# Attention stage of a graph network: slot rows laid out group by group, whole-tile stores, SyncE's steps reordered, PSUM banks shared out anew

## The reference, cut to what matters

```python
q = (embeds[rows] @ qW).reshape(e, HEADS, dh)
k = (embeds[cols] @ kW).reshape(e, HEADS, dh)
v = (embeds[cols] @ vW).reshape(e, HEADS, dh)
scores = jnp.clip(jnp.einsum('ehd,ehd->eh', q, k), -10.0, 10.0)
exp_s = jnp.exp(scores)
norms = jax.ops.segment_sum(exp_s, rows, num_segments=nvar)[rows]
w = exp_s / (norms + 1e-08)
res = jax.ops.segment_sum(w[:, :, None] * v, rows, num_segments=nvar).reshape(nvar, d)
return embeds + res
```

## Time and profile before

| | us |
|---|---|
| median of 3 runs | 4100.52 (4100.29 to 4103.03) |
| profiled execution | 4099.22 |
| its span | 4097.9 |
| TensorE busy, weight loads busy | 3879.6, 3664.7 |
| VectorE, ScalarE, GpSimd busy | 1806.4, 1328.4, 518.4 |
| attention stage, from and to | about 283 to 1194 |

### The profile page before, as it was taken

One profiled execution on the slowest core, in us unless ns is written; L12 is line 12 of the kernel. 1 busy time (PEld: TensorE's weight loads), 2 busy tenths in 40 slices (PEclk: granted clock), 3 DMA queues, 4 the chain that ended last, 5 costly groups with the idle time before them and its releaser, 6 DMA issues.

```text
span 4097.9 us, 125285 instructions
## 1 busy us (share of the span) xinstructions
PE 3879.6 (95%) x46211; PEld 3664.7 (89%) x46211; DVE 1806.4 (44%) x4350; ACT 1328.4 (32%) x3904; POOL 518.4 (13%) x708
## 2 busy tenths in 40 slices
PE   3779999999979999899999999999999998999999
PEld 2669999999966665899999999999999998999998
DVE  8988999999984332322222222222222222331121
ACT  1237777777773111122222222222222221111110
POOL 1015555555530000000000000000000000000000
PEclk9989999999989999999999999999999999999999
DMA  1029999999983332555555555555555655566674
GB/s 40 3 60 216 222 220 220 219 220 222 221 212 108 108 109 81 179 203 202 204 203 201 205 202 201 205 201 202 205 201 201 207 200 192 189 219 210 212 217 145
DMA packets 525196, 746.41 MB, mean 182 GB/s; under 512 B 203503, under 2 KB 449647, under 8 KB 525036
## 3 DMA queue, kind: packets, MB, share of 16 engines
q1 hardware_dynamic: 520040, 743.21, 60.8%
q10 hardware_dynamic: 4996, 0.88, 0.1%
HBM read 620.51 MB, written 83.32 MB: 172 GB/s over the span
## 4 chain that ended last, share of the span: by engine, by line
PE 71%; DVE 9%; SPq 7%; issue 5%; DMA 5%; ACT 1%; POOL 1%; DVEq 0%; ACTq 0%; POOLq 0%
PE sum L1647 48%; PE sum L1340 19%; DMA rows<-slot_rows_d 5%; SPq L960 3%; DVE onerank L759 2%; SPq L967 1%; SPq L956 1%; DVE sc L993 1%; POOL sc L1063 1%; PE l L465 1%; SPq L943 1%; DVE qk L986 1%; PE pk L1111 1%; DVE bt L731 1%; DVE prodb L748 1%
## 5 line engine op out<-in xcount | busy, mean ns | idle before, releaser
L1647 PE MATMUL sum<-y,ring 128*128 128x192 f16 x12005 | 995.0, 246 | 4.0 <-ACT y L1496 4.0
L1647 PEld LDWEIGHTS sum<-y,ring 128*128 128x128 fp8e4 x12005 | 993.8, 98 | 4.6 <-issue 4.2
L1647 PE MATMUL sum<-u2b,ring 128*128 128x192 f16 x12005 | 993.0, 246 | 0.0
L1647 PEld LDWEIGHTS sum<-u2b,ring 128*128 128x128 fp8e4 x12005 | 992.1, 98 | 0.2
L1656 DVE TENSOR_TENSOR z<-lo,sum 128x96 f32<-128x96 f32 x441 | 112.1, 254 | 1004.5 <-ACT lo L1671 1004.0
L1111 PE MATMUL pk<-kv,hT 128*128 128x192 f16 x4900 | 486.3, 247 | 11.4 <-DVE hT L1005 9.7
L1340 PE MATMUL sum<-u,ring 128*128 128x385 f16 x2401 | 402.7, 328 | 22.2 <-ACT u L1464 22.2
L1111 PEld LDWEIGHTS pk<-kv,hT 128*128 128x128 f16 x4900 | 410.2, 99 | 12.7 <-DVE hT L1005 9.6
L1340 PEld LDWEIGHTS sum<-u,ring 128*128 128x128 fp8e4 x2401 | 235.7, 98 | 182.5 <-issue 24.6
L1192 ACT ACTIVATE kvs<-pk 128x384 f32<-128x384 f32 x735 | 313.6, 437 | 154.4 <-PE pk L1111 149.8
L1134 PE MATMUL pr<-wv,hs_wide 128*128 128x101 f32 x2450 | 323.6, 279 | 15.0 <-ACT sums L1199 13.8
(11 more groups left out here) (237 smaller groups left out, 3369.7 us busy)
## 6 DMA issues: line engine op xcount, KB each, us to landing
ring<-adjacency_t SPq DMA_DIRECT2D x490, 800.0 KB, 4.3
ring<-adjacency SPq DMA_DIRECT2D x147, 896.0 KB, 4.7
rows<-slot_rows_d SPq DMA_DIRECT2D x245, 320.0 KB, 4.0
adjacency<-row SPq DMA_DIRECT2D x147, 128.0 KB, 3.6
adjacency_t<-col SPq DMA_DIRECT2D x147, 128.0 KB, 2.6
adjacency<-row SPq DMA_DIRECT2D x49, 256.0 KB, 3.6
adjacency_t<-col SPq DMA_DIRECT2D x49, 256.0 KB, 2.4
adjacency<-row SPq DMA_DIRECT2D x49, 160.0 KB, 3.7
```

Of the source, the lines that this page charges most:

```text
L1647: m = pe.matmul(ps[r][:, 0:2 * D], w[:, t // 2, :, t % 2], n["this"][:, t, 0:2 * D], start=t == 0, stop=t == TILES - 1)
```

## The change

- Slot rows lie in DRAM and in SBUF group by group: 128 source places, then 128 destination places of a group. A chunk's load is then one run of 2560 bytes in DRAM.
- The one-hots hT are made from a pattern with gaps; reading and writing go over two halves of each group (`halves`).
- The matrices of a tile are stored whole, one DMA each for `adjacency` and `adjacency_t`, in place of five each; the transposes stay one for each chunk.
- SyncE transposes chunk c-7 (before: c-3) and stores a turned tile at lag 9 (before: its parts at lag 5); its loop has a lag of 9.
- pk has three banks in place of two, pq two in place of one. Keys and values of one third of a chunk have their own bank, and `query` waits for the score product of chunk e-2 in place of e-1.
- ScalarE copies the sums ahead of the keys and values of its step.

```diff
@@ -851,7 +851,7 @@
             x0, x1 = x_halves[h]
             n0 = 2 * x0 + i * (x1 - x0)
             eng.wait_ge(k.rows_sb.sem, k.rows_sb.at(-(-2 * x1 // 8)))
-            to = k.rows_d.rearrange("(x t) i (g e) -> t i g x e", t=2, e=P)
+            to = k.rows_d.rearrange("(x t) g i e -> t i g x e", t=2)
             for odd in range(2):
                 eng.dma_start(to[odd, i][:, x0:x1, :], k.slot_rows[odd * GROUPS:(odd + 1) * GROUPS, n0:n0 + x1 - x0, :]
                               ).then_inc(k.rows_out[h].sem, 16)
@@ -881,7 +881,7 @@
     k.weighted, k.summed = Beat(k, "at_weighted", CP), Beat(k, "at_summed", CP)
     k.q_in, k.denom, k.inverse, k.normed = (Beat(k, f"at_{x}", 2) for x in ("q_in", "denom", "inverse", "normed"))
     k.ratio, k.totalled = (Beat(k, f"at_{x}", 2) for x in ("ratio", "totalled"))
-    k.row_out, k.col_out = ([Beat(k, f"at_{x}{c}", n) for c in range(CHUNKS)] for x, n in (("row_out", 64), ("col_out", 32)))
+    k.row_out, k.col_out = ([Beat(k, f"at_{x}{b}", n) for b in range(2)] for x, n in (("row_out", 16 * CHUNKS + 16), ("col_out", 16)))
     k.out_c = Beat(k, "at_out_c", 2 * UP)
     k.av_set = k.sig("av_set")
 
@@ -894,13 +894,13 @@
 
 
     v, a, pe, pool, sp = k.v, k.a, k.pe, k.pool, k.sp
-    rows = [k.buf(ctx, f"rows{i}", [P, 2, CHUNK * P], F16) for i in range(HOMES)]
+    rows = [k.buf(ctx, f"rows{i}", [P, CHUNK, 2, P], F16) for i in range(HOMES)]
     ss = [k.buf(ctx, f"ss{i}", [P, 4, GROUPS, 2], BF16) for i in range(2)]
     high_d = [k.buf(ctx, f"high_d{i}", [P, GROUPS, HIGH_D, 2], BF16) for i in range(2)]
     low_d = [k.buf(ctx, f"low_d{i}", [P, GROUPS, LOW_D // 2, 2], BF16) for i in range(2)]
     highs, lows = k.buf(ctx, "highs", [P, HIGH_D, 2], BF16), k.buf(ctx, "lows", [P, LOW_D // 2, 2], BF16)
     q2 = [k.buf(ctx, f"q2_{i}", [P, 2, D], F16) for i in range(2)]
-    hT = [k.buf(ctx, f"hT{i}", [P, 3, CHUNK * P], F16) for i in range(2)]
+    hT = [k.buf(ctx, f"hT{i}", [P, 3, CHUNK, P], F16) for i in range(2)]
     hs = [k.buf(ctx, f"hs{i}", [P, CHUNK, P // 2, 2], BF16) for i in range(2)]
     hs_wide = [k.buf(ctx, f"hs_wide{i}", [P, CHUNK, P], F32) for i in range(HOMES)]
     hd = [k.buf(ctx, f"hd{i}", [P, CHUNK, HIGH_D, LOW_D // 2, 2], BF16) for i in range(2)]
@@ -915,10 +915,11 @@
     rowsum = k.buf(ctx, "rowsum", [P, TILES * UP], F32)
     bits = k.buf(ctx, "bits", [P, TILES * UP], I32)
     most = k.buf(ctx, "most", [P, 2], F32)
-    pq, pr = k.bank(ctx, "pq"), k.bank(ctx, "pr")
-    pk = [k.bank(ctx, f"pk{i}") for i in range(2)]
+    pr = k.bank(ctx, "pr")
+    pq = [k.bank(ctx, f"pq{i}") for i in range(2)]
+    pk = [k.bank(ctx, f"pk{i}") for i in range(3)]
     pc = [k.bank(ctx, f"pc_{i}") for i in range(2)]
-    LAG = 5
+    LAG, SENT, SP_LAG = 5, 7, 9
     last_tiles = TILES - 2 * (PAIRS - 1)
     last_chunks = last_tiles * CHUNKS
 
@@ -936,46 +937,44 @@
                 for g in range(g1 - CHUNK, g1) if g % BANK == BANK - 1 or g == GROUPS - 1]
 
     def load_rows(X, e):
-        b, i, at = e // CHUNKS, e % HOMES, (e % CHUNKS) * CHUNK * P
+        b, i, g0 = e // CHUNKS, e % HOMES, (e % CHUNKS) * CHUNK
         sp.wait_ge(k.turned.sem, k.turned.at(X, e - HOMES))
         k.settle(sp)
-        src = k.rows_d[2 * X + b, :, at:at + CHUNK * P]
-        sp.dma_start(rows[i][:], src.partition_broadcast(P)).then_inc(k.rows_in[i].sem, 16)
-
-    def parts(e):
-
-        u = units(e)
-        return e // CHUNKS, u[0][1], u[-1][1] + u[-1][2], u[-1][0]
-
-    def send(X, e):
-
-        b, g0, g1, u = parts(e)
-        c = e % CHUNKS
-        sp.wait_ge(k.out_c.sem, k.out_c.at(X, u))
+        src = k.rows_d[2 * X + b, g0:g0 + CHUNK, :, :].rearrange("g i e -> (g i e)")
+        sp.dma_start(rows[i][:].rearrange("p g i e -> p (g i e)"), src.partition_broadcast(P)).then_inc(k.rows_in[i].sem, 16)
+
+    def turn_counts(X, e):
+
+        b, u = e // CHUNKS, units(e)
+        g0, g1 = u[0][1], u[-1][1] + u[-1][2]
+        if e % CHUNKS == 0:
+            sp.wait_ge(k.col_out[b].sem, k.col_out[b].at(X, -1))
+            k.settle(sp)
+        sp.wait_ge(k.out_c.sem, k.out_c.at(X, u[-1][0]))
         k.settle(sp)
-        sp.dma_start(k.c_d[2 * X + b, :, g0 * GROUP:g1 * GROUP],
-                     flat(row[b][:, g0:g1, :]).bitcast(U8)).then_inc(k.row_out[c].sem, 16)
-        sp.wait_ge(k.col_out[c].sem, k.col_out[c].at(X, 16 * b - 1))
+        sp.dma_start_transpose(col[b][:, g0:g1, :], flat(row[b][:, g0:g1, :])).then_inc(k.row_out[b].sem, 16)
+
+    def store(X, b):
+
+        sp.dma_start(k.c_d[2 * X + b, :, :], flat(row[b][:]).bitcast(U8)).then_inc(k.row_out[b].sem, 16)
+
+    def store_turned(X, b):
+        sp.wait_ge(k.row_out[b].sem, k.row_out[b].at(X, 16 * CHUNKS + 15))
         k.settle(sp)
-        sp.dma_start_transpose(col[b][:, g0:g1, :], flat(row[b][:, g0:g1, :])).then_inc(k.row_out[c].sem, 16)
-
-    def send_transposed(X, e):
-        b, g0, g1, _ = parts(e)
-        c = e % CHUNKS
-        sp.wait_ge(k.row_out[c].sem, k.row_out[c].at(X, 32 * b + 31))
-        k.settle(sp)
-        sp.dma_start(k.t_d[2 * X + b, :, g0 * GROUP:g1 * GROUP],
-                     flat(col[b][:, g0:g1, :]).bitcast(U8)).then_inc(k.col_out[c].sem, 16)
+        sp.dma_start(k.t_d[2 * X + b, :, :], flat(col[b][:]).bitcast(U8)).then_inc(k.col_out[b].sem, 16)
 
     def sync_step(X, c, first=False, chunks=CP):
         if first and c == LAG - 1:
             sp.wait_ge(k.rows_out[1].sem, k.rows_out[1].at(64))
         for x, e in lagged(X, c, 0, first, chunks):
             load_rows(x, e)
-        for x, e in lagged(X, c, 3, first, chunks):
-            send(x, e)
-        for x, e in lagged(X, c, 5, first, chunks):
-            send_transposed(x, e)
+        for x, e in lagged(X, c, SENT, first, chunks):
+            turn_counts(x, e)
+            if e % CHUNKS == CHUNKS - 1:
+                store(x, e // CHUNKS)
+        for x, e in lagged(X, c, SP_LAG, first, chunks):
+            if e % CHUNKS == CHUNKS - 1:
+                store_turned(x, e // CHUNKS)
 
     def score(X, e):
         i = e % 2
@@ -983,7 +982,7 @@
             v.wait_ge(k.kv_out.sem, k.kv_out.at(X, 3 * e + n))
         v.wait_ge(k.queried.sem, k.queried.at(X, e))
         v.wait_ge(k.summed_qk.sem, k.summed_qk.at(X, e - 2))
-        v.tensor_tensor(qk[i][:].rearrange("p (g d) -> p g d", d=D), pq[:, 0:CHUNK * D].rearrange("p (g d) -> p g d", d=D),
+        v.tensor_tensor(qk[i][:].rearrange("p (g d) -> p g d", d=D), pq[i][:, 0:CHUNK * D].rearrange("p (g d) -> p g d", d=D),
                         kv[i][:, :, 0:D], ALU.mult).then_inc(k.scored.sem, 1)
 
     def score_sum(X, e):
@@ -992,17 +991,21 @@
         v.wait_ge(k.exped.sem, k.exped.at(X, e - 2))
         v.tensor_reduce(sc[i][:], qk[i][:].rearrange("p (h d) -> p h d", d=DH), AX.X, ALU.add).then_inc(k.summed_qk.sem, 1)
 
+    def halves(ap):
+
+        return ap.rearrange("p g (h e) -> p h g e", h=2)
+
     def turn_source(X, e):
         i, h = e % 2, e % HOMES
         v.wait_ge(k.taken.sem, k.taken.at(X, 3 * (e - 2) + 2))
         v.wait_ge(k.queried.sem, k.queried.at(X, e - 2))
         v.wait_ge(k.rows_in[h].sem, k.rows_in[h].at(X, 16 * (e // HOMES) + 15))
-        v.tensor_scalar(hT[i][:, 0, :], rows[h][:, 0, :], k.pid[:, 0:1], None, ALU.is_equal)
+        v.tensor_scalar(halves(hT[i][:, 0, :, :]), halves(rows[h][:, :, 0, :]), k.pid[:, 0:1], None, ALU.is_equal)
 
     def turn_destination(X, e):
         i, h = e % 2, e % HOMES
         for m in range(2):
-            t = v.tensor_scalar(hT[i][:, 1 + m, :], rows[h][:, 1, :], k.dpid[:, m:m + 1], None, ALU.is_equal)
+            t = v.tensor_scalar(halves(hT[i][:, 1 + m, :, :]), halves(rows[h][:, :, 1, :]), k.dpid[:, m:m + 1], None, ALU.is_equal)
         t.then_inc(k.turned.sem, 1)
 
     def factors(X, e):
@@ -1105,22 +1108,22 @@
         for g in of:
             n, place = g // 2, (g % 2) * 2 * D
             if g % 2 == 0:
-                pe.wait_ge(k.kv_out.sem, k.kv_out.at(X, 3 * e + n - 2))
+                pe.wait_ge(k.kv_out.sem, k.kv_out.at(X, 3 * e + n - 3))
             for m in range(2):
                 for part in range(2):
-                    t = pe.matmul(pk[(3 * e + n) % 2][:, place:place + 2 * D], hT[i][:, 1 + m, g * P:(g + 1) * P],
+                    t = pe.matmul(pk[n][:, place:place + 2 * D], hT[i][:, 1 + m, g, :],
                                   k.kv[:, 2 * (g0 + g) + m, part, :], start=m == part == 0, stop=m == part == 1)
             if g % 2 == 1 or g == CHUNK - 1:
                 t.then_inc(k.taken.sem, 1)
 
     def query(X, e):
         b, i = e // CHUNKS, e % 2
-        pe.wait_ge(k.scored.sem, k.scored.at(X, e - 1))
+        pe.wait_ge(k.scored.sem, k.scored.at(X, e - 2))
         if e % CHUNKS == 0:
             pe.wait_ge(k.q_in.sem, k.q_in.at(X, b))
         for g in range(CHUNK):
             for part in range(2):
-                t = pe.matmul(pq[:, g * D:(g + 1) * D], hT[i][:, 0, g * P:(g + 1) * P], q2[b][:, part, :],
```

(30 more changed lines are left out.)

## The result

The changed kernel takes **4059.9 us** (median, 4058.78 to 4061.58), the kernel before 4100.67 beside it; the ratio is 0.990, 95% interval 0.9888 to 0.9912. The forecast was 4068 with a range of 4046 to 4089. The profiled execution's span is 4057.7 us, 40.2 less than before.

What follows compares the result with a forecast made beforehand. VectorE, waiting for slot rows in the attention stage, was taken as the bound, TensorE close behind. 4099.2 - 35.3 (stage) + 2.7 (its end) = 4066.6, the median 1.3 above: 4068 us, range 4046 to 4089.

Steps and rivals of the forecast that it cites:

- What bounds: Attention stage: VectorE, waiting 59.2 us for slot rows, sets the pace at 18.64 us a tile; TensorE is busy 17.49.
- Loads ahead, all 59.2 us of waits gone: SyncE's slot-row loads go out some 14 us before use, so VectorE's 59.2 us of waits for rows vanish.
- What is given back beside wv: hT at L1000 stalls while GpSimd's wv runs, so removed waits partly return; 35.3 us gained over 49 tiles.
- The bound by 79 waits: VectorE's hT: 79 waits each give back at most 0.38 us, 30.0 of 59.2; window gain 29.2 to 59.2.
- the last chunk of a tile: VectorE, from one score product to the next in that chunk: 3.98 us before, 3.46 forecast.
- TensorE's three edits: Second query bank (27.0 us of waits), sums copied first (21.7), third key-value bank (0 to 5.7): worth nothing alone, needed together.
- The sum of 17.92: VectorE's five chunks of a tile: 3.46 + 5.19 + 2.81 + 3.23 + 3.23 us, against 18.64 before.
- Halves: VectorE's hT read as two halves stays at 0.37 us, costing nothing; at 0.48 it would cost 81 us.
- Layout and packets: Slot-row loads and tile stores in longer runs and fewer DMAs: costed at nothing; two to three SyncE issues saved a chunk.
- The end of the stage: After the last evacuation, the turned store waits for the whole-tile store to land: 2.7 us later, all on the path.
- TensorE as the bound: Rival: no stall beside wv in the attention stage, TensorE's 825.6 us is the floor; 4045 to 4057 us, chance 0.17.
- The lock with wv: VectorE's hT stands still while GpSimd's wv runs; rival that this moves to hd: 4077 to 4090 us, chance 0.15.

Runs made afterwards that it cites:

- the two edits: Kernel before with SyncE's loads issued earlier (lags 7 and 9): 4091.83 us; kernel before with two pq banks, three pk banks, sums copied first: 4105.33 us.
- SyncE's order alone: Kernel before with only SyncE's lags changed to 7 and 9; parts, layout and banks as before: 4091.83 us, ratio 0.9966.
- both together: Kernel before with SyncE's lags 7 and 9, two pq banks, three pk banks and sums copied first; old layout, ten stores a tile: 4058.84 us.
- the slower hT: Changed kernel with the sources' hT read as five gapped rows into one run: 4050.27 us; with the last tile also stored in two parts: 4049.27 us.
- the gapped read: Changed kernel with all three hT of a chunk made from five gapped rows into one run, without halves: 4093.41 us, ratio 0.9972.

## Why the prediction was right, point by point

- **What bounds.** Right: VectorE with its waits for rows, and TensorE close behind. That the two edits are worth 13 and 0 us apart and 46 together shows it. Only TensorE's edits were called worth nothing alone, and they were. For SyncE's order alone, the prediction's 18.52 us a tile against 18.64 makes 6 us; 13 were won, at 18.45.
- **Loads ahead, all 59.2 us of waits gone.** Right, and by the late issue: the old lags bring 44.0 back in spite of the longer packets, and with the new lags and the old packets (both together) there is no wait for rows either.
- **What is given back beside wv.** The mechanism is right. The bound by 79 waits, 30.0 us, was passed in the rows of the line, where 35.5 came back. The stall is 0.78 - 0.37 = 0.41 us and not 0.38, which makes 32.4; the rest was not traced. The gain in the window, 40.0 us, lies within the 29.2 to 59.2 of this bound. The term that was mis-sized is the last chunk of a tile, 3.46 forecast and 3.32 measured. Its pause of some 0.15 us between the reciprocal and L986 was in the row of before and I kept it; it is gone. It was a wait for keys and values. In the row of before, ScalarE's last copy of them ended at 649.96, 0.19 us ahead of L986; in the rows after, it ends at 649.71, 0.76 ahead of L985 (before, then after):

```profile
649.63 0.33 ACT L1192 ACTIVATE kvs<-pk 128x192 f32<-128x192 f32 x1 [0.26 <-PE pk L1111]
...
648.43 1.28 ACT L1196 ACTIVATE kvs<-pk 128x384 f32<-128x384 f32 x3
```

With any one of TensorE's three edits undone it is 0.19 to 0.20 again, and the chunk takes 3.46 to 3.55. So the statement that none of the three shortens VectorE's part failed here by 0.15 us a tile. The sum of 17.92 was 17.77, so 0.15 x 49 = 7.4 us too high. The mean of before, 18.64, was right.
- **TensorE's three edits.** Two query banks and the sums are needed, as said: undone they cost about 9 and 11 us. The third key-value bank was sized at 0 to 5.7 us from the idle time of before, and is worth 8.3. The step that failed is to bound a wait by a trace in which something else held it off.
- **Halves.** Right: hT stays at 0.37 us. Without them it takes 0.54, where I had bounded it by hs with 0.48. The rule of the Trainium skill ("VectorE: DVE Perf Modes", section "Mode 2×_2P — use both read ports for one tensor") told the sign: five rows into one run fail it, two halves do not, and both hT rows agree.
- **Layout and packets.** Right: nothing. (The issues saved at SyncE are 8 a tile, 1.6 a chunk and not two to three; nothing hung on it.)
- **The end of the stage.** 2.7 us forecast, 1.8 measured. The store landed in 4.6 us, as taken; the turned store in 3.3 (1157.78 to 1161.11), where I took 4.2. The estimate by the Trainium skill, "DMA: Bandwidth & Descriptors", section "Anatomy of one DMA", was 1.6, so its sum was nearer, but partly by luck. The section gives its fit for DMAs that GpSimd issues, and these are SyncE's; of the 3.9 us for each store, one took 4.6 and the other 3.3.
- **The rivals.** TensorE as the bound did not come with the change, but it is what the slower hT brings, at 4049 to 4050. The lock with wv, as the prediction calls the standing still, did move to another instruction once a tile (hs in place of hd, 1.30 against 1.29), and cost nothing new. In place of TensorE's waits for pq and pr the prediction looked for a few short ones for hT; the few that came are at pk and, for ScalarE's copy of the queries, at pq (5.9 and 4.3 us). The whole error of 8 us is 7.4 + 0.9 from the last chunk and the end.

## What to carry to other kernels

Where two engines of a stage are both within a few per cent of its time, remove both of their waits or expect little; a part tried alone and found worthless may be needed. A load's lead is set by what its queue waits for before it, so put long waits of the issuing queue behind the loads. And what a wait of VectorE covers is worth a look before it is removed: here 35.5 of 59.2 us came back in one instruction that stood beside GpSimd, and the slower form of the instruction that stood was the better choice.

## What was not expected of the hardware

- The 16-bit comparison of 640 elements takes 0.37 us in two halves or in one run, 0.54 us from five gapped rows into one run. Beside GpSimd's wv the first takes 0.78 and the second still 0.54. Whether this instruction stands still for GpSimd thus goes with its rate, and is set by the shape of its pattern.
- tensor_tensor with both inputs in SBUF stood for wv as well: hs or hd 1.30 in place of 0.48, low_d 1.15 in place of 0.36. The qk product, with one input in PSUM, and the reduce did not (0.64 with or without wv).
- GpSimd stood still for VectorE as well. Its clip (L1066) took 0.77 us on average in the changed kernel, beside the hT of the destinations in halves, and 0.35 beside the gapped ones. Its wv took 1.00 when it started beside the qk product. With the gapped read it started in the middle of hs in four chunks of five, and took 1.46 on average. The changed kernel first, then the gapped read:

```profile
L1066 POOL TENSOR_SCALAR sc<-sc,bound 128x20 f32<-128x20 f32 x236 | 182.4, 773 | 238.0 <-DVE sc L992 237.5
L1071 POOL TENSOR_TENSOR wv<-kvs,wv 128x480 f32<-128x480 f32 x236 | 246.1, 1043 | 103.0 <-ACT wv L1176 103.0
```

```profile
L1066 POOL TENSOR_SCALAR sc<-sc,bound 128x20 f32<-128x20 f32 x227 | 80.2, 353 | 264.0 <-DVE sc L992 260.1 <-issue 3.9
L1071 POOL TENSOR_TENSOR wv<-kvs,wv 128x480 f32<-128x480 f32 x228 | 333.9, 1464 | 108.3 <-ACT wv L1176 108.3
```

- A DMA share of 1.03 of the stage in the kernel with short packets went with no wait for rows at all. This share did not tell how near the DMA engines were to a limit.
